# A selective scan and a quantized layer in one pass: softplus as one ScalarE function, the output summed in memory, and parts of two normalisations on GpSimd

## The reference

```python
def _layernorm(x, axis=-1, eps=1e-05):
    m = jnp.mean(x, axis=axis, keepdims=True)
    v = jnp.var(x, axis=axis, keepdims=True)
    return (x - m) / jnp.sqrt(v + eps)

# step 1: selective scan with 16 states, rank 64
A = -jnp.exp(A_log)
xp = jnp.einsum('bld,ed->ble', x, x_proj_w)
delta = jax.nn.softplus(jnp.einsum('blr,dr->bld', xp[..., :64], dt_proj_w) + dt_proj_b)
deltaA = jnp.exp(jnp.einsum('bld,dn->bldn', delta, A))
deltaB_u = jnp.einsum('bld,bln,bld->bldn', delta, Bm, x)
h = dA_t * h + dBu_t          # over l
y = jnp.einsum('bdn,bn->bd', h, C_t)   # + x * D

# step 2: a layer quantized to 8 bits
x_scale = jnp.maximum(max|x2d|, 1e-6) / 127.0
x_q = clip(round(x2d / x_scale), -128, 127)
out = (x_q @ weight_q.T) * x_scale * weight_scale + bias
```

## Time and profile before

| | before |
|---|---|
| median of 3 runs | 3097.05 us (3096.6 to 3104.22) |
| the profiled execution | 3105.25 us |
| its span | 3103.4 us |
| VectorE busy | 2978.6 us (96%) |
| ScalarE busy | 2952.2 us (95%) |
| TensorE busy | 2800.9 us (90%) |
| GpSimd busy | 2766.5 us (89%) |
| moved by the DMA engines | 236.01 MB, mean 76 GB/s |

### The profile page before, as it was taken

One profiled execution on the slowest core, in us unless ns is written; L12 is line 12 of the kernel. 1 busy time (PEld: TensorE's weight loads), 2 busy tenths in 40 slices (PEclk: granted clock), 3 DMA queues, 4 the chain that ended last, 5 costly groups with the idle time before them and its releaser, 6 DMA issues.

```text
span 3103.4 us, 57860 instructions
## 1 busy us (share of the span) xinstructions
PE 2800.9 (90%) x21569; PEld 2423.8 (78%) x21632; DVE 2978.6 (96%) x3234; ACT 2952.2 (95%) x4930; POOL 2766.5 (89%) x1488
## 2 busy tenths in 40 slices
PE   5899999999999999999999899998999998999986
PEld 4778878788877788777887777887778877878875
DVE  5999999999999999999999999999999999999996
ACT  7999999999999999999999999999999999999984
POOL 3899989899899988999889998999889998899987
PEclk8999999999999999999999999999999999999998
DMA  4221222221222212222212222122222122221111
GB/s 151 66 79 56 79 80 79 80 92 42 80 92 79 79 57 79 79 79 93 79 43 79 93 79 79 58 78 80 79 82 91 42 82 90 79 79 66 56 65 41
DMA packets 111225, 236.01 MB, mean 76 GB/s; under 512 B 56097, under 2 KB 56097, under 8 KB 94562
## 3 DMA queue, kind: packets, MB, share of 16 engines
q1 hardware_dynamic: 110946, 232.32, 21.4%
HBM read 195.92 MB, written 36.37 MB: 75 GB/s over the span
## 4 chain that ended last, share of the span: by engine, by line
PE 31%; DVE 30%; ACT 29%; issue 9%; POOL 1%; DVEq 0%; POOLq 0%; ACTq 0%
DVE A L635 23%; ACT A L400 12%; ACT DB L413 10%; PE PB L519 9%; PE Y L538 9%; PE PB L516 6%; PE PM L559 3%; DVE ST L650 2%; DVE X L640 2%; ACT Z L465 2%; ACT QT L491 1%; ACT Z L461 1%; PE PM L550 1%; ACT C L483 1%; DVE AM L676 1%
## 5 line engine op out<-in xcount | busy, mean ns | idle before, releaser
L359 POOL TENSOR_TENSOR A<-A,CB 128x2048 f32<-128x2048 f32 x512 | 2327.9, 4560 | 17.8 <-DVE A L635 5.6
L635 DVE TENSOR_TENSOR_SCAN A<-A,CAR,PB 128x512 f32<-128x512 f32 x1536 | 1871.9, 1262 | 36.0 <-PE PB L519 12.5
L400 ACT ACTIVATE A<-DEL,an 128x512 f32<-128x512 f32 x2048 | 1366.5, 711 | 4.6 <-PE Y L538 3.0
L519 PE MATMUL PB<-idf,DB 128*128 128x128 f32 x6656 | 1030.7, 280 | 183.7 <-DVE A L635 175.1
L538 PE MATMUL Y<-idf,A 128*128 128x128 f32 x8192 | 1129.0, 275 | 2.0 <-POOL A L359 2.0
L413 ACT ACTIVATE DB<-XN,BC 128x512 f32<-128x512 f32 x1664 | 1113.1, 710 | 4.8 <-PE PB L519 2.7
L519 PEld LDWEIGHTS PB<-idf,DB 128*128 128x128 f32 x6656 | 768.8, 143 | 425.4 <-DVE A L635 306.3
L538 PEld LDWEIGHTS Y<-idf,A 128*128 128x128 f32 x8192 | 954.8, 143 | 32.6 <-issue 16.4
L635 DVE TENSOR_TENSOR_SCAN A<-A,PB 128x512 f32<-128x512 f32 x512 | 596.9, 1204 | 34.2 <-PE PB L519 14.4
L516 PE MATMUL PB<-DG,XN 128*128 128x128 f32 x3072 | 421.9, 281 | 50.9 <-DVE A L635 48.0
L516 PEld LDWEIGHTS PB<-DG,XN 128*128 128x128 f32 x3072 | 372.2, 191 | 87.1 <-issue 51.2
(11 more groups left out here) (69 smaller groups left out, 1678.3 us busy)
## 6 DMA issues: line engine op xcount, KB each, us to landing
CB<-c_rows SPq DMA_DIRECT2D x128, 1024.0 KB, 4.8
X<-in_x SPq DMA_DIRECT2D x32, 1024.0 KB, 5.6
out<-X SPq DMA_DIRECT2D x32, 1024.0 KB, 4.3
DG<-b_diag SPq DMA_DIRECT2D x32, 768.0 KB, 6.9
b_diag<-DG SPq DMA_DIRECT2D x2, 768.0 KB, 9.3
b_diag<-BC SPq DMA_DIRECT2D x96, 2.0 KB, 5.1
C<-in_wq SPq DMA_DIRECT2D x1, 1024.0 KB, 11.5
DB<-in_wq SPq DMA_DIRECT2D x1, 1024.0 KB, 13.3
```

What stands on the lines that cost most here:

```text
L359: gp.tensor_tensor(A[s % NA][:, :, :], A[s % NA][:, :, :], CB[:, s % (4 * NG), :].unsqueeze(1).broadcast_to([128, KB, L]), ALU.mult).then_ ...
L400: act.activation(A[s % NA][:, g, :], DEL[k % 2][:, g, :], ACT.Exp, scale=an[:, g, n:n + 1])\
L519: i = pe.transpose(PB[u % 2][:, j * 128:(j + 1) * 128], DB[(scaled(s) - 1) % ND][:, j, g * 128:(g + 1) * 128], idf[:, :])
L635: dve.tensor_tensor_scan(A[s % NA][:, g, :], A[s % NA][:, g, :], PB[(4 * s + g) % 2][:, :], init, ALU.mult, ALU.add).then_inc(s_scan, 1)
```

## The change

Four things change together, and all places are written anew.

- Softplus is one ScalarE function, read from the bank and written to DEL. `z_out`, `sp_exp`, `sp_ln`, VectorE's `delta` and the tile Z are gone.
- `root` and `newton` become `rstd` on GpSimd: a power of -0.5.
- `centre` (LN2's normalisation) moves from ScalarE to GpSimd.
- `addbias`, `final` and `store` are gone. SP's `put_bias` writes the bias rows to the output, and GpSimd issues two transfers that add to it: `add_x` adds X once `gather` is done, `add_c` adds C once `scale_out` is done. `load` waits for `add_x` and `centre` of the chunk that had the buffer.

```diff
@@ sync
             def load(p):
                 i = p % NX
                 if p >= NX:
-                    sp.wait_ge(s_out[i], 16 * (p // NX))
+                    sp.wait_ge(s_ax[(p - NX) % 2], 16 * ((p - NX) // 2 + 1))
+                    sp.wait_ge(s_c, T * (p - NX + 1))
...
-            def store(p):
-                sp.wait_ge(s_fin, T * (p + 1))
-                sp.dma_start(of[p * L:(p + 1) * L, :].rearrange("(t p) d -> p t d", p=128), X[p % NX][:, :, :])\
-                  .then_inc(s_out[p % NX], 16)
+            def put_bias(p):
+                if p == 0:
+                    sp.wait_ge(s_w2, 64)
+                sp.dma_start(of[p * L:(p + 1) * L, :].rearrange("(t p) d -> p t d", p=128),
+                             bib[:, :].unsqueeze(1).broadcast_to([128, T, D])).then_inc(s_bi[p % 2], 16)
@@ gpsimd
-            def newton(p, w):
...
+            def rstd(p, w):
+                m, sm, c0 = MV[w], SM[w], 4 * p
+                gp.wait_ge(s_ag[w], T * (p + 1))
+                if p >= 1:
+                    gp.wait_ge(s_c if w else s_xn, T * p)
+                gp.tensor_scalar(sm[:, 0, :], m[:, :, 1], 1e-5, 1.0, ALU.add, ALU.mult).then_inc(s_rs[w], 1)
+                gp.tensor_scalar(sm[:, 1, :], m[:, :, 0], -1.0, 1.0, ALU.mult, ALU.mult).then_inc(s_rs[w], 1)
+                gp.wait_ge(s_rs[w], c0 + 2)
+                gp.tensor_tensor(sm[:, 2, :], sm[:, 0, :], mhalf[:, :], ALU.pow).then_inc(s_rs[w], 1)
+                gp.wait_ge(s_rs[w], c0 + 3)
+                gp.tensor_tensor(sm[:, 3, :], sm[:, 2, :], sm[:, 1, :], ALU.mult).then_inc(s_rs[w], 1)
...
-            def addbias(p):
...
-            def final(p, h):
...
+            def centre(p, j):
+                if j == 0:
+                    gp.wait_ge(s_rs[1], 4 * p + 4)
+                    gp.wait_ge(s_wb, 2)
+                    if p >= 1:
+                        gp.wait_ge(s_ac[(p - 1) % 2], 16 * ((p - 1) // 2 + 1))
+                gp.tensor_scalar(C[:, j, :], X[p % NX][:, j, :], SM[1][:, 2, j:j + 1], SM[1][:, 3, j:j + 1],
+                                 ALU.mult, ALU.add).then_inc(s_c, 1)
+
+            def add_x(p):
+                gp.wait_ge(s_y, T * (p + 1))
+                gp.wait_ge(s_bi[p % 2], 16 * (p // 2 + 1))
+                gp.dma_start(of[p * L:(p + 1) * L, :].rearrange("(t p) d -> p t d", p=128), X[p % NX][:, :, :],
+                             accum_op=ALU.add).then_inc(s_ax[p % 2], 16)
+
+            def add_c(p):
+                gp.wait_ge(s_o, T * (p + 1))
+                gp.wait_ge(s_ax[p % 2], 16 * (p // 2 + 1))
+                gp.dma_start(of[p * L:(p + 1) * L, :].rearrange("(t p) d -> p t d", p=128), C[:, :, :],
+                             accum_op=ALU.add).then_inc(s_ac[p % 2], 16)
@@ scalar
-            def root(p, w):
...
-            def z_out(p, g):
...
-            def sp_exp(p, g):
...
-            def sp_ln(p, g):
...
-            def centre(p, j):
...
+            def delta(p, g):
+                act.wait_ge(s_dt, KB * p + g + 1)
+                if g == 0 and p >= 2:
+                    act.wait_ge(s_exp, 4 * NS * (p - 1))
+                    act.wait_ge(s_dlt, T * (p - 1))
+                act.activation(DEL[p % 2][:, g, :], bank(p, g)[:, :], ACT.Softplus).then_inc(s_del, 1)
@@ vector
-            def delta(p, g):
...
```

More of the change, by code:

```diff
@@ L25 @@
-        "du": (-111, -98, -79, -67),
-        "final": (1721, 1733),
-        "gather": (1166, 1180, 1181, 1257),
-        "load": (-2168,),
-        "load_c": (139, 170, 249, 288),
-        "load_g": (-148,),
-        "magic": (1374, 1391, 1403, 1434),
-        "newton0": (-1221,),
-        "newton1": (1151,),
-        "q_mm": (1566, 1663, 1700, 1736),
-        "q_t": (1411, 1434, 1462, 1524),
-        "qt_out": (1423, 1446, 1472, 1495),
-        "root0": (-1296,),
-        "root1": (1220,),
-        "scale_out": (1626, 1669, 1709, 1733),
@@ new lines @@
+        220, 268, 300, 314, 338, 353, 363, 382, 385, 387, 408, 427, 438, 473, 560, 601, 622, 625, 634, 654,
+        658, 666, 669, 672, 714, 719, 746, 763, 766, 792, 863, 921),
+        "add_c": (2111,),
+        "add_x": (1592,),
+        "amax": (1358, 1423, 1458, 1504),
+        "ascale": (1580,),
+        "b_c": (-449,),
+        "bc_out": (-467,),
+        "carry": (75, 217, 288, 341, 416, 500, 516, 584, 604, 674, 696, 744, 833, 841, 977, 1058),
+        "centre": (1405, 1411, 1461, 1535),
@@ new lines @@
+        "gather": (1068, 1131, 1168, 1171),
+        "load": (-3287,),
+        "load_c": (-941, -936, -810, -775),
+        "load_g": (-1166,),
+        "magic": (1569, 1633, 1645, 1680),
+        "put_bias": (-946,),
+        "q_mm": (1846, 1896, 2056, 2070),
+        "q_t": (1605, 1722, 1752, 1801),
+        "qt_out": (1668, 1682, 1697, 1734),
+        "rstd0": (-1295,),
+        "rstd1": (1393,),
+        "scale_out": (1821, 1924, 1994, 2035),
+        "scales": (1507,),
+        "scan": (-44, -27, -26, -15, 29, 46, 50, 51, 68, 105, 106, 119, 122, 123, 135, 163, 169, 178, 242,
@@ L149, in build @@
         s_xl = [sem(f"s_xl{i}") for i in range(NX)]
-        s_out = [sem(f"s_out{i}") for i in range(NX)]
         s_cst = sem("s_cst")
@@ L175, in build @@
         s_rs = [sem(f"s_rs{i}") for i in range(2)]
-        s_lv = [sem(f"s_lv{i}") for i in range(2)]
-        s_nw = [sem(f"s_nw{i}") for i in range(2)]
         s_xn = sem("s_xn")
@@ L200, in build @@
         s_o = sem("s_o")
-        s_yb = sem("s_yb")
-        s_fin = sem("s_fin")
+        s_bi = [sem(f"s_bi{i}") for i in range(2)]
+        s_ax = [sem(f"s_ax{i}") for i in range(2)]
+        s_ac = [sem(f"s_ac{i}") for i in range(2)]
         block = ctx.enter_context(nc.Block())
```

157 lines of the change are left out of this document (44 added, 113 removed), and 16 rows, old and new, of the table PLACES.

## The result

The changed kernel takes 2986.68 us (median of 4 runs, 2986.22 to 2987.45), the kernel before 3097.02 in the same measurement: ratio 0.9633, with an interval of 0.9616 to 0.965. That is 3.7% faster. The profiled execution took 2986.22 us. A kernel's time is compared here with that of the kernel before in the same measurement (the ratio), and that one's median lay between 3097 and 3108 us; differences in us against 2986.68 are between measurements and good to a few us only.

A forecast was written before the change was run, and what follows sets the result against it. VectorE was taken to bound the kernel: 31 periods x 2.34 = 72.6 us, with 5 and less 1.9, made 75.7 off 3105.25, so 3029.5; less 8.2 for the slower profiled execution, 3021 us, range 2990 to 3090.

The forecast's parts named there:

- The start and the end: Outside the middle periods: earlier softplus in chunk 0 gives -5.2 us, the changed tail sums to +1.9 us.
- VectorE's saving: On VectorE, each chunk loses four maximum-and-add steps of 0.58 us, 2.3 us, and gains nothing.
- If the 1.87 us of idle time stay, the period is 92.4 us: In the middle, VectorE's busy time falls to 90.5 us a chunk; with its idle time unchanged the period is 92.4.
- So VectorE sets the period: In the middle, VectorE is idle only 1.87 of 94.73 us a chunk, with ScalarE 0.7 us behind it.
- These 7.8 us are worth nothing by themselves: ScalarE's saving of 7.8 us a chunk, to 84.3, gives no time since ScalarE is no longer close to last.
- counted in the range: TensorE, with idle down to 5.3 us and two PB banks, can be late for a scan more often; no separate term.
- rival 2: Half the gain is eaten by GpSimd at its upper bound or by too little TensorE idle: 3045 to 3085 us, chance 0.16.
- the bound of 0.93: On GpSimd, one power step of the new sequences costs 0.19 to 0.93 us, priced at 0.28.
- 1 (GpSimd late, issue at 6.5 us or more): Costly transfer issues make GpSimd last, slower than now from 6.5 us each; 3190 us at 8 us, chance 0.09.
- rival 4: Nothing measurable changes, since several small losses meet: chance 0.08.
- 3 (eight loads a chunk): On ScalarE, a table load before and behind each of four softplus, 10.3 us a chunk: 3173 us, chance 0.05.
- the new wait: VectorE's maxima now wait for GpSimd's centrings; with 12 us of room a chunk, GpSimd was expected in time.

The follow-up runs named there:

- b_no_dve_delta: The kernel before, own order, without VectorE's four softplus-finishing steps a chunk (Ln writes DEL directly): 3095.99 us, ratio 0.997.
- b_one_step: The kernel before, own order, with one ScalarE step (Abs) for softplus, so VectorE's step and ScalarE's Exp and Ln are gone: 3095.04 us, ratio 0.998.
- b_no_exp_ln: The kernel before, own order, without ScalarE's Exp and Ln of softplus, VectorE's step kept: 3098.98 us, ratio 0.9988.
- o_all: The changed kernel's work, with Abs for softplus, at the places of the kernel before: 3207.32 us, ratio 1.0333.
- the kernel with all three edits: The changed kernel with maxima over 8 columns, Abs in place of Softplus and a third PB bank: 2939.02 us, ratio 0.9461.

## Why the prediction was right and wrong

**The start and the end** were right (-3.1 forecast, -3.1 measured), though the terms of the end differ. The sequence on GpSimd takes 2.1 us there (2958.64 to 2960.74), not 1.1, and the four centrings 3.03, not 3.7. From the last `scale_out` (2974.51) to the end are 10.0 us, where 7.9 + 2.3 = 10.2 was forecast.

**VectorE's saving** was right in size (2.34 us a chunk forecast; its busy time fell by 2.65). The same four steps taken away in `b_no_dve_delta`, where waits grew, lowered it by 1.97, so the difference seems to go with the waits (a step behind a wait doesn't overlap with the one before it); that is a reading, not shown.

**The step that failed** is "If the 1.87 us of idle time stay, the period is 92.4 us". It stood on "So VectorE sets the period". Both are wrong for the old order, and the first for the new one. In the old order the idle time didn't stay but grew to 3.8 us, as `b_one_step` showed, and the same saving was worth 0.15 us. In the new order it shrank to 0.93. The account of the 3.69 us a chunk, as the runs give it: softplus's relief in the old order 0.15 to 0.3, the order at nearly the old load about 0.7 (the size of the half-clock stretches that go with it), and the remaining 2.7 only from relief and order together. The diff showed that every place had been written anew, and the prediction costed the parts and took the lists as neutral. That the time came within 1.2% of the forecast is partly luck: the same sum would have stood for the relief in the old order, where it gave almost nothing.

**"These 7.8 us are worth nothing by themselves"** was right in the old order (`b_no_exp_ln`: 0.1 us) and wrong in the new one: 3.5 of the 7.8 put back cost 43.6 us. ScalarE at 86.7 of 91.1 us busy looks as if it had 4.4 us of room. It has some, since 2.6 us of table loads cost nothing there, but it is used up within the next 3.5 us.

**TensorE**, put at an unchanged 87.05 us, is busy 86.06, since its clock no longer falls in the middle (PEclk 0.99 before, 1.00 after); the prediction had no term for the clock. Its lateness was only "counted in the range", and the text took "VectorE waits for TensorE and ScalarE hardly at all" as evidence against rival 2. The waits before, shown above, had the sign that was needed: 105.8 us of TensorE waiting for VectorE on the same banks on which VectorE waited 13.8. With the earlier trace rows I had read GpSimd's waits alone.

**ScalarE.** Softplus takes 593 ns (0.50 by starts where nothing waits), the forecast's price. The table is foreign, and there are exactly two loads a chunk, 32 + 32 (`L449`, `L398`). They were forecast free and are. Chunk 0 shows what a switch takes, on ScalarE's timeline after:

```profile
30.40 0.60 ACT L449 ACTIVATE DEL<-Y 128x512 f32<-128x512 f32 x1 [0.26 <-PE Y L548]
...
31.02 1.28 ACT L398 ACT_TABLE_LOAD   x1
...
32.31 1.95 ACT L398 ACTIVATE A<-DEL,an 128x512 f32<-128x512 f32 x3
```

The load follows the softplus after 0.02 us and the next step follows the load after 0.01, and it is so at all 64. ScalarE is at 86.72, which agrees with the forecast of 86.9 from rows alone. The rule cited from the Trainium skill, ScalarE: Activation LUTs, section "What ACT_TABLE_LOAD costs", of a drain of 1.38 us beside the load does not show here as time; by that estimate ScalarE would have been at 89.6.

**GpSimd** was forecast at 82.6 us and stands at 83.69. Within that, the power takes 1.04 us, above the bound of 0.93 that I gave it (I bounded a new function by a scalar step of 512 columns, for four elements a row); centring takes 0.74 us by starts, not 0.93. The two errors cancel in part: 2 x (1.04 - 0.28) = +1.5 and 4 x (0.74 - 0.93) = -0.8, which leaves +0.7 of the 1.1 us; the rest isn't traced. The issue was put at 1.5 and takes 1.35. GpSimd's timeline after:

```profile
1226.95 0.20 POOL L340 COPY CAR<-A 128x4 f32<-128x4 f32 x1
1227.09 1.35 POOL L376 DMA_DIRECT2D out<-C  x1
1227.98 5.04 POOL L349 TENSOR_TENSOR A<-A,CB 128x2048 f32<-128x2048 f32 x1
1232.48 0.67 POOL L340 COPY CAR<-A 128x4 f32<-128x4 f32 x1
1233.23 4.55 POOL L349 TENSOR_TENSOR A<-A,CB 128x2048 f32<-128x2048 f32 x1
```

The pass behind the issue takes 5.04 us where its neighbour takes 4.55. Its start (1227.98) lies inside the issue's 1.35 us, so half a us of the issue is seen a second time in it; the copy behind it is long too (0.67, not 0.20). By starts the issue costs 0.9 us up to the next pass and 0.5 in that pass, 1.4 in all, the forecast's price. With the rule cited from the Trainium skill, Perfetto Trace Analysis, section "DMA Instruction — SWDGE (GPSIMD)", that the descriptors are written by GpSimd's own processors, the trace agrees in that the issue is 1.35 us of busy time of the engine. The size lies in the lower part of the bounds (0.38 to 4.5), though, and no run changed the number of pieces.

**The rivals.** 1 (GpSimd late, issue at 6.5 us or more) needs an issue five times what it is, and 2.3 us more on GpSimd costs 5. 2 (half the gain eaten) named TensorE, which is what eats the relief in the old order, and there it eats nearly all of it (`b_one_step`, 0.998), as rival 4 had it; in the changed kernel neither came. 3 (eight loads a chunk) is excluded by the count of two. The mechanism of the new wait is real: it appears as soon as the places are wrong (98.14 us).

**What stays open.** Which of ScalarE and the banks is nearer in the new order: the runs show both within 0.6 us and no finer. What the whole relief would give in the old order with the centrings well placed: the one kernel that has it, `o_all`, has the wait for GpSimd in it. How much of the 0.7 us is owed to the order (or to the clock with it), and how much to where I put the dummy work, which doesn't stand where the old work stood. Whether a kernel in the old order with an undisturbed clock runs at the 94.0 us estimated above: none was made with two banks. Why adding 2.3 us costs 2.1 and taking 2.0 away gives 0.4 is explained by several limits at one height, which the kernel with all three edits supports; whether the height was reached by the way the list was made wasn't tried. None of the kernels here computes the layer and is faster than the changed kernel.

## What to carry to other kernels

An engine that is 98% busy in a hand-ordered program isn't shown to set the period: look on both sides of each small set of buffers, and if both engines wait there (here 105.8 and 13.8 us of 1500), relief on one can turn into waiting unless the lists or the number of buffers change with it. Look at the granted clock beside it, since an engine that waits there can come back at half speed (13 times in 24 chunks before, in none of the same chunks after). Price a diff that rewrites the order as two changes, the work and the places, and expect the work's saving to need the places. And where a new order has brought several engines to one height, added work can cost much of its size (here 2.1 of VectorE's 2.3 us and 1.4 of ScalarE's 3.5, but 0.1 of GpSimd's 2.3) while removed work gives little (0.4 of VectorE's 2.0).
